# Second matmuls of the last feed-forward: from one pass per token tile behind four gelus to one pass per block right behind its gelu

## The chip, the cores and the metric

The kernel runs on one core of a Trainium2 chip. The metric is the device time of one launch in microseconds (us); lower is better. The inputs and outputs lie in the chip's memory.

## What is computed

The reference is a stack of two gated layers on 4 x 1024 tokens of 256 features. Only its last two steps bear on the change:

```
x = x + jnp.tanh(g_xattn[1]) * _L1_xattn_ref(_layernorm(x, axis=-1), ctx_1024, ctx_1024)
x = x + jnp.tanh(g_ffn[1]) * _L1_ffn_ref(_layernorm(x, axis=-1), ...)
```

The first is softmax attention of 16 heads (depth 16) over 154 keys. The second is a feed-forward whose butterfly stages are linear, so the kernel folds them into its two weight matrices ahead of time:

```
h = jnp.einsum('bsd,dh->bsh', x, W_exp) + b_exp     # 256 -> 1024
h = butterfly(h, up_weights, D_HIDDEN)
h = jax.nn.gelu(h + up_bias, approximate=False)
h = butterfly(h, down_weights, D_HIDDEN)
y = jnp.einsum('bsh,hd->bsd', h, W_con) + b_con     # 1024 -> 256
return y + down_bias
```

What is left of it is y = gelu(x A + a) C + c with A 256 x 1024 and C 1024 x 256. The 1024 hidden units are 8 blocks of 128.

## The kernel before

Five engines each run their own program; they meet at semaphores. There are three stages (first attention, experts, last), and this text is about the last, which fills the span from about 870 us on. It works on halves: h = 0 to 7, each of 512 tokens (4 tiles of 128). x stays on the chip, and each half is updated in place.

All five programs walk one list of units, made by `plan_last`. Its clock is a position n = 20 h + c. At every position one 128 x 512 block of attention weights of half h is made: `scores1` (TensorE, into one of the score banks of PSUM), `exp1` (ScalarE, `ACTIVATE`, L1124), and after every five of them `weigh1` (L652, L647), a ScalarE copy, and `normalize1` (L881, L1536 to L1541). `scores1` of n + 2 is issued at position n and waits for the exp of n - 1, since three banks take turns. Beside that, `beside(h, c)` adds at fixed c:

- the next half's preparation: `peak` units (16 in a half, two PSUM banks each; L846 and L848 on TensorE, then two maxima of 128 x 308 on VectorE, L1521), `peaks` (their transposition, L856), and for h + 2 its layer norm, `turn_q1` and `send_q1`;
- the feed-forward of half h - 1: layer norm `f` (L1180, L1183, L1221 on VectorE, L1621 on GpSimd), `turn_f`, then at c = 9 and at c = 19 a **burst** of four `up` units (hidden blocks 0 to 3 and 4 to 7). Each `up` is six 512-column matmuls (L898: two halves of the contraction times three products of high and low parts), a gelu on ScalarE (L1152), a cast on VectorE (L1569) and a subtraction on GpSimd (L1668) that yield the high and the low part of the hidden block;
- the second matmuls, `out`: one unit per token tile t, 12 matmuls of 256 columns (L911: four blocks times three products) into a bank of its own, and one VectorE addition into x (L1578). They stand at c = 12 to 15 for the burst at 9, and at c = 1 to 4 of the next half for the burst at 19. The first of them waits for the low part of all four blocks.

PSUM banks 4 to 7 are a ring, `wide`, which `peak`, `up`, `out` and the transpositions share in the order of the list. Hidden blocks have four buffers, and the gelu's own output two (`whole`), so the gelu of a block waits for the subtraction of the block two before it. Names of tiles in the trace: `hidden_whole` is `whole`, `hidden` the two parts, `peaks` the maxima, `q_stack` and `k_stack` the stacked queries and keys.

The feed-forward of half 7 stands behind all attention (positions 160 and on); there nothing is left beside it.

## Time and profile before

| what | value |
|---|---|
| median of 3 runs | 1425.98 us (1422.92 to 1426.78) |
| profiled execution, own time | 1429.87 us |
| its span | 1428.1 us |
| TensorE busy | 1148.7 us, 80% |
| VectorE busy | 823.9 us, 58% |
| ScalarE busy | 739.4 us, 52% |
| GpSimd busy | 380.0 us, 27% |
| mean granted TensorE clock | 0.883 of full speed |

The busy times are sums over the whole span, so they hide that the stages have different limits: in the last stage one has to see which engine is waited for in each stretch between two bursts. A granted clock of 1.00 is 2.4 GHz and of 0.50 is 1.2 GHz; a mean between them is the share of either.

### The profile page before, as it was taken

Reading aid. Unit: us, or ns where it says so; the run is one execution under the profiler, and the core shown is the slowest. Engines: PE = TensorE matmul, PEld = TensorE weight load, DVE = VectorE, ACT = ScalarE, POOL = GpSimd, SP = SyncE. Lnnn points to the kernel's source line nnn. Section 1 sums busy time; section 2 is a strip of 40 time slices with the busy share of each in tenths; the row PEclk is TensorE's granted clock in tenths of the full one; section 3 lists DMA queues with packets and bytes.
Section 4 is the critical chain, followed back from the end, with each engine's and each line's share of the span. In section 5 each row is a group of like instructions: output and inputs, shape, how many; then the busy total and the mean of one; then the engine's idle time right before and its main releaser. Section 6 shows DMA issues by size and latency. Waiting matters only on the chain.

```text
span 1428.1 us, 18332 instructions
## 1 busy us (share of the span) xinstructions
PE 1148.7 (80%) x6049; PEld 842.0 (59%) x6049; DVE 823.9 (58%) x2068; ACT 739.4 (52%) x1469; POOL 380.0 (27%) x320
## 2 busy tenths in 40 slices
PE   4788888787774667999699961769888888989887
PEld 3354543543333456888588861637766666767566
DVE  4386687777765554455645434657565565755342
ACT  2786677777862643556656521343443435334521
POOL 3011011011000001566556552103323242321422
PEclk9697999999996999999999995597989998999988
DMA  8214414504103103677557745330403123020000
GB/s 251 78 63 118 115 60 118 173 18 128 51 34 138 71 1 95 157 164 178 169 141 168 187 71 142 98 93 2 112 20 89 43 70 93 17 60 3 15 15 15
DMA packets 89900, 129.77 MB, mean 91 GB/s; under 512 B 20496, under 2 KB 59792, under 8 KB 89552
## 3 DMA queue, kind: packets, MB, share of 16 engines
q1 hardware_dynamic: 77520, 109.73, 25.8%
q0 software_dynamic: 12288, 18.88, 7.6%
q8 instruction: 49, 0.80, 0.2%
q14 instruction: 43, 0.35, 0.1%
HBM read 72.18 MB, written 30.70 MB: 72 GB/s over the span
## 4 chain that ended last, share of the span: by engine, by line
PE 58%; DVE 17%; ACT 10%; issue 5%; DMA 3%; SPq 3%; POOL 3%; POOLq 0%; ACTq 0%; DVEq 0%
PE psum L911 8%; PE psum L741 6%; PE psum L652 5%; PE psum L817 4%; PE psum L629 3%; PE psum L757 3%; PE psum L846 3%; PE psum L776 3%; PE psum L647 3%; PE psum L898 3%; POOL hidden L1668 3%; SPq L1725 2%; PE psum L826 2%; PE psum L618 2%; DVE weights L1281 2%
## 5 line engine op out<-in xcount | busy, mean ns | idle before, releaser
L629 PE MATMUL psum<-q_stack,k_stack 96*128 96x512 f32 (+1 forms) x256 | 130.2, 525 | 70.9 <-ACT weights L1124 29.3
L1616 POOL TENSOR_SCALAR vareps<-moments 128x4 f32<-128x4 f32 x32 | 8.3, 260 | 517.0 <-DVE moments L1183 517.0
L1668 POOL TENSOR_TENSOR hidden<-hidden_whole,hidden 128x512 fp32r<-128x512 f32 x64 | 83.8, 1316 | 203.0 <-DVE hidden L1569 203.0
L1521 DVE TENSOR_REDUCE peaks<-psum 128x2 f32<-128x308 f32 x256 | 105.5, 468 | 46.1 <-PE psum L848 46.0
L1649 POOL DMA_INDIRECT expert_sums<-made,sum_rows x64 | 102.9, 1607 | 101.2 <-DVE made L1491 85.2
L846 PE MATMUL psum<-k_stack,q_stack 96*128 96x256 f32 x256 | 97.6, 443 | 33.9 <-DMA q_stack<-q_stage 11.0
L911 PE MATMUL psum<-w_con_high,hidden 128*128 128x256 f32 x512 | 114.2, 322 | 10.6 <-POOL hidden L1668 10.5
L629 PEld LDWEIGHTS psum<-q_stack,k_stack 96*128 96x128 f32 (+1 forms) x256 | 52.8, 211 | 116.9 <-DVE weights L1281 46.7
L652 PE MATMUL psum<-weights,values 128*32 128x512 f32 x512 | 106.4, 701 | 10.3 <-DVE weights L1281 10.3
L1124 ACT ACTIVATE weights<-psum 128x512 f32<-128x512 f32 x160 | 88.9, 602 | 47.9 <-PE psum L632 23.9
L1281 DVE SCALAR_TENSOR_TENSOR weights<-psum,weights 128x512 f32<-128x512 f32 x160 | 107.1, 679 | 5.4 <-ACT weights L982 5.0
L1641 POOL DMA_INDIRECT got<-rows_scratch,tokens x64 | 70.2, 1097 | 142.5 <-DVE sum_rows L1478 123.3
L1569 DVE CAST hidden<-hidden_whole 128x512 fp32r<-128x512 f32 x64 | 51.1, 799 | 95.1 <-ACT hidden_whole L1152 94.0
L911 PEld LDWEIGHTS psum<-w_con_high,hidden 128*128 128x128 f32 x512 | 91.9, 218 | 23.6 <-POOL hidden L1668 12.6
L982 ACT ACTIVATE weights<-weights 128x512 f32<-128x512 f32 x160 | 101.2, 632 | 1.0
L977 ACT ACTIVATE weights<-weights 128x512 f32<-128x512 f32 x160 | 100.4, 628 | 0.1
L741 PE MATMUL psum<-feat_parts,w_shared_up 128*128 128x512 f32 x384 | 98.4, 406 | 0.0
L846 PEld LDWEIGHTS psum<-k_stack,q_stack 96*128 96x128 f32 x256 | 59.4, 232 | 63.0 <-issue 40.0
L969 ACT ACTIVATE weights<-psum 128x512 f32<-128x512 f32 x128 | 75.9, 593 | 12.2 <-PE psum L629 7.3
L741 PEld LDWEIGHTS psum<-feat_parts,w_shared_up 128*128 128x128 f32 x384 | 71.8, 194 | 14.4
L911 PE MATMUL psum<-w_con_low,hidden 128*128 128x256 f32 x256 | 78.7, 307 | 0.0
L898 PE MATMUL psum<-feats,w_up_high 128*128 128x512 f32 x256 | 77.1, 414 | 1.7 <-DVE feats L1561 1.7
(187 smaller groups left out, 2646.2 us busy)
## 6 DMA issues: line engine op xcount, KB each, us to landing
q_stack<-q_stage SPq DMA_DIRECT2D x192, 128.0 KB, 2.4
expert_w<-in_expert_w SPq DMA_DIRECT2D x64, 384.0 KB
expert_sums<-zeros SPq DMA_DIRECT2D x6, 1408.0 KB, 7.1
fetched<-expert_sums SPq DMA_DIRECT2D x16, 512.0 KB, 4.6
wk_stack<-in_wk SPq DMA_DIRECT2D x16, 384.0 KB, 3.8
rows_scratch<-rows SPq DMA_DIRECT2D x8, 640.0 KB, 3.4
k_raw<-in_k SPq DMA_DIRECT2D x16, 300.0 KB
x<-in_x SPq DMA_DIRECT2D x8, 512.0 KB, 6.7
```

What stands on the lines that cost most here:

```text
L629: T.matmul(to, k[0:row, head, :], q[0:row, head // 2, :], start=True, stop=True).then_inc(scored, 1)
L652: m = T.matmul(to[32 * j:32 * j + 32, :], vals[:, 0, 4 * g + j, :], w[(n + j) % len(w)][:, :], start=True, stop=False, tile_position=(0, 3 ...
L741: m = T.matmul(misc.ap(key, half), w_sgu[:, pw, a:a + P], sh_parts[:, pf, c * HALF:(c + 1) * HALF], start=n == 0 and c == 0, stop=n == 2 a ...
L846: T.matmul(view[:, :, 0:P], q[0:STACK, p, t * P:(t + 1) * P], keys[0:STACK, 2 * p:2 * p + 2, :], start=True, stop=True)
L898: m = T.matmul(wide.ap(key), up_parts[pw][:, c, k * P:(k + 1) * P], feats[:, pf, c, :], start=i == 0 and c == 0, stop=i == 2 and c == CD - 1)
L911: m = T.matmul(wide.ap(key)[:, 0:DIM], hidden[k][:, ph, t * P:(t + 1) * P], con_parts[pw][:, BURST * b + k, :], start=k == 0 and q == 0, s ...
L977: A.activation(weights[n % 9][:, :], weights[n % 9][:, :], ACT.Ln, bias=1.0, scale=1.0 if on_act else -1.0).then_inc(logged, 1)
L982: A.activation(weights[n % 9][:, :], weights[n % 9][:, :], ACT.Exp, scale=-1.0).then_inc(exped, 1)
L1281: V.scalar_tensor_tensor(weights[n % 9][:, :], score_bank[n % 5], 1.0, weights[n % 9][:, :], ALU.add, ALU.max).then_inc(weighted, 1)
L1521: V.tensor_reduce(peaks[h % 2][:, t, 2 * p:2 * p + 2], view, AX.X, ALU.max).then_inc(wide.frees(key, i), 1)
L1649: G.indirect_dma_start(sum_dram[e % SUMS], bass.IndirectOffsetOnAxis(ap=sum_rows[:, e:e + 1], axis=0), made[e % 4][:, :], None, bounds_che ...
L1668: G.tensor_tensor(hidden[k % BURST][:, 1, :], whole[n % 2][:, :], hidden[k % BURST][:, 0, :].bitcast(F32), ALU.subtract).then_inc(hid_spli ...
```

## The change

The unit `out` is now (h, b, k): block k of burst b, all four token tiles, 12 matmuls that wait only for that block's low part. The four tiles are summed over the four blocks in two banks of their own (3 and 4), two tiles to a bank, and VectorE adds each bank to x in one instruction of 128 x 512 when all four blocks are in. The banks come from two places: the score banks go from three to two, so `scores1` now runs one position ahead instead of two (`scores1` of n + 1 at position n, which still waits for the exp of n - 1), and the ring `wide` goes from four to three. `burst` interleaves a burst on TensorE: up 0, up 1, up 2, out 0, up 3, out 1, out 2, out 3. In the burst at c = 9 three of the 16 `peak` units stand between its pieces. `out` units no longer stand at c = 12 to 15 and 1 to 4; `peaks` moves from c = 12 to 13; the list is one half shorter.

```diff
-PEAKS_AT = (1, 1, 1, 1, 2, 1, 2, 2, 1, 3, 1)
+PEAKS_AT = (1, 1, 1, 1, 1, 1, 1, 2, 4, 1, 1, 1)
+
+
+def burst(h, b, between):
+
+    up, out = [("up", h, BURST * b + k) for k in range(BURST)], [("out", h, b, k) for k in range(BURST)]
+    between = [[u] for u in between] + [[]] * 4
+    return up[:2] + between[0] + [up[2], out[0]] + between[1] + [up[3], out[1]] + between[2] + [out[2], out[3]]
...
-        if c == 12:
+            peak = peak[sum(PEAKS_AT[:c - 1]):sum(PEAKS_AT[:c])]
+            units, peak = (units + peak[:1], peak[1:]) if c == 9 else (units + peak, [])
+        if c == 13:
             units.append(("peaks", h + 1))
...
         if c in (9, 19):
-            units += [("up", h - 1, c // 10 * BURST + k) for k in range(BURST)]
-        if 12 <= c < 12 + HT:
-            units.append(("out", h - 1, 0, c - 12))
-    if 2 <= h <= HALVES + 1 and 1 <= c <= HT:
-        units.append(("out", h - 2, 1, c - 1))
-    return units
+            return units + burst(h - 1, c // 10, peak)
+    return units + peak
...
-    for n in range(20 * (HALVES + 2)):
+    for n in range(20 * (HALVES + 1)):
...
-        if n + 2 < len(CHUNKS):
-            plan.append(("scores1", n + 2))
+        if n + 1 < len(CHUNKS):
+            plan.append(("scores1", n + 1))
...
-        score_bank, o_bank, o_bank1 = bank[0:5], bank[5], bank[3]
+        score_bank, o_bank, o_bank1, out_bank = bank[0:5], bank[5], bank[2], bank[3:5]
...
-        wide = Ring(bank[4:8], sems("wide_full", 4), sems("wide_free", 4))
+        wide = Ring(bank[5:8], sems("wide_full", 3), sems("wide_free", 3))
...
-                attention_scores(n, FIRST, 3, exped, q1_stack, k1_stack, ROWS1)
+                attention_scores(n, FIRST, 2, exped, q1_stack, k1_stack, ROWS1)
...
+            def out_part(h, b, k):
+                n = BURST * (2 * h + b) + k
+                if h == 0 and k == 0:
                     T.wait_ge(con_split, 4 + b + 1)
...
+                T.wait_ge(hid_split, n + 1)
+                for t in range(HT):
+                    if k == 0 and t % 2 == 0 and n:
+                        T.wait_ge(out_added, n // BURST * 2 - 1 + t // 2)
                     for q, (ph, pw) in enumerate(PRODUCTS):
...
+                        m = T.matmul(out_bank[t // 2][:, t % 2 * DIM:(t % 2 + 1) * DIM],
+                                     hidden[k][:, ph, t * P:(t + 1) * P], con_parts[pw][:, BURST * b + k, :],
+                                     start=k == 0 and q == 0 and t % 2 == 0,
+                                     stop=k == BURST - 1 and q == 2 and t % 2 == 1)
+                m.then_inc(out_made, 1)
...
+            def out_add(h, b, k):
+                if k == BURST - 1:
+                    n = 2 * h + b
+                    if b == 0:
+                        V.wait_ge(out_biased, h + 1)
+                    V.wait_ge(out_made, BURST * (n + 1))
+                    for two in range(HT // 2):
+                        xs = x[:, HT * h + 2 * two:HT * h + 2 * two + 2, :].rearrange("p i f -> p (i f)")
+                        if b:
+                            V.wait_ge(out_added, 2 * n - 1 + two)
+                        V.scalar_tensor_tensor(xs, out_bank[two], tg[:, 3:4], xs, ALU.mult,
+                                               ALU.add).then_inc(out_added, 1)
```

The first place is TensorE's burst at c = 19 of half 3 and what follows it (`feats` and `w_up` are the operands of `up`, `hidden` and `w_con` those of `out`, `q_stack` those of scores, `k_stack` of peaks). Before:

```order
L898 MATMUL psum<-feats,w_up_high 128x512 x4
L898 MATMUL psum<-feats,w_up_low 128x512 x2
L898 MATMUL psum<-feats,w_up_high 128x512 x2
L629 MATMUL psum<-q_stack,k_stack 128x512
L647 MATMUL psum<-weights_1,values_1 128x512
L629 MATMUL psum<-q_stack,k_stack 128x512
L846 MATMUL psum<-k_stack,q_stack 128x2x128
L848 MATMUL psum<-k_stack,q_stack 128x2x26
L846 MATMUL psum<-k_stack,q_stack 128x2x128
L848 MATMUL psum<-k_stack,q_stack 128x2x26
L911 MATMUL psum<-w_con_high,hidden 128x256 x2
L911 MATMUL psum<-w_con_low,hidden 128x256
```

After, from the last block of the same burst (lines 898, 911, 629, 647, 846 and 848 are now 903, 916, 634, 652, 851 and 853):

```order
L903 MATMUL psum<-feats,w_up_high 128x512 x2
L903 MATMUL psum<-feats,w_up_low 128x512 x2
L903 MATMUL psum<-feats,w_up_high 128x512 x2
L916 MATMUL psum<-w_con_high,hidden 128x256 x2
L916 MATMUL psum<-w_con_low,hidden 128x256
...
L634 MATMUL psum<-q_stack,k_stack 128x512
L652 MATMUL psum<-weights_1,values_1 128x512
L634 MATMUL psum<-q_stack,k_stack 128x512
L851 MATMUL psum<-k_stack,q_stack 128x2x128
L853 MATMUL psum<-k_stack,q_stack 128x2x26
```

Before, scores and weighing followed the four `up` units at once, and the second matmuls came behind them between `peak` units; now all second matmuls of the burst stand ahead of the next scores, and no second matmul follows until the next burst.

The second place is VectorE from the burst at c = 19 (the casts) to the one at c = 9 of the next half. Before:

```order
L1569 CAST hidden<-hidden_whole 128x512 x4
L1521 TENSOR_REDUCE peaks<-psum 128x2 x2
L1578 SCALAR_TENSOR_TENSOR x<-psum,tanh_gates,x 128x256
L1536 RECIPROCAL sums_1<-psum 128x16
L1538 TENSOR_TENSOR att_1<-psum,sums_1 128x256
L1541 SCALAR_TENSOR_TENSOR x<-att_1,tanh_gates,x 128x4x64
L1521 TENSOR_REDUCE peaks<-psum 128x2 x2
L1180 BN_STATS stats<-x 128x6 x4
L1183 BN_AGGR moments<-stats 128x2 x4
```

After:

```order
L1575 CAST hidden<-hidden_whole 128x512 x4
L1587 SCALAR_TENSOR_TENSOR x<-psum,tanh_gates,x 128x512 x2
L1527 TENSOR_REDUCE peaks<-psum 128x2 x2
L1542 RECIPROCAL sums_1<-psum 128x16
L1544 TENSOR_TENSOR att_1<-psum,sums_1 128x256
L1547 SCALAR_TENSOR_TENSOR x<-att_1,tanh_gates,x 128x4x64
L1527 TENSOR_REDUCE peaks<-psum 128x2 x2
L1186 BN_STATS stats<-x 128x6 x4
L1189 BN_AGGR moments<-stats 128x2 x4
```

The four additions of 128 x 256 that stood between maxima are two of 128 x 512 ahead of all of them, behind the burst's last matmul.

## Rows read from the trace of the kernel before

**Rows 1.** Who TensorE waited for, 980 to 1368 us: total us, times, longest.

```profile
PE psum L629 <- ACT weights L1124: 25.9, 13, 3.0
PE psum L846 <- DVE peaks L1521: 9.1, 11, 1.2
```

**Rows 2.** Timeline around a burst at c = 19: start, us, engine, line, idle before.

```profile
1134.10 0.73 PE L898 MATMUL psum<-feats,w_up_high 128*128 128x512 f32 x2
1135.84 1.28 ACT L1152 ACT_TABLE_LOAD   x1 [2.72 <-PE psum L898]
1138.43 1.29 POOL L1668 TENSOR_TENSOR hidden<-hidden_whole,hidden 128x512 fp32r<-128x512 f32 x1 [13.37 <-DVE hidden L1569]
1139.77 0.40 PE L629 MATMUL psum<-q_stack,k_stack 100*128 100x512 f32 x1
1144.04 0.50 PE L629 MATMUL psum<-q_stack,k_stack 100*128 100x512 f32 x1 [3.01 <-ACT weights L1124]
```

**Rows 3.** Busy us of each engine in stretches, then granted clock, DMA share.

```profile
core 0: us, PE busy (x) PEld busy (x) DVE busy (x) ACT busy (x) POOL busy (x), PEclk, DMA share, GB/s
926.00:952.00 26.00, 20.52 (x117) 13.11 (x117) 21.62 (x52) 13.75 (x25) 2.02 (x2) 0.99 0.09 26
960.00:977.00 17.00, 16.25 (x60) 12.26 (x61) 11.05 (x31) 3.87 (x8) 7.76 (x5) 0.50 0.20 65
1083.00:1106.00 23.00, 21.96 (x139) 17.27 (x139) 17.46 (x47) 6.10 (x12) 8.35 (x5) 0.89 0.12 40
1106.00:1119.50 13.50, 11.83 (x52) 9.40 (x52) 8.12 (x14) 7.28 (x10) 5.10 (x4) 0.88 0.00 1
1119.50:1134.00 14.50, 13.45 (x92) 10.06 (x89) 9.01 (x25) 5.79 (x11) 1.27 (x2) 0.94 0.02 5
1134.00:1144.00 10.00, 7.03 (x31) 5.00 (x27) 4.31 (x4) 5.82 (x8) 4.49 (x4) 1.00 0.74 174
1144.00:1168.00 24.00, 22.87 (x142) 17.94 (x142) 17.61 (x47) 6.78 (x13) 8.97 (x6) 0.88 0.32 92
1182.00:1197.50 15.50, 14.45 (x90) 11.01 (x88) 11.40 (x28) 7.37 (x13) 2.00 (x2) 0.87 0.14 42
```

**Rows 4.** VectorE groups (last row: 980 to 1378 us): count, busy, mean ns.

```profile
L1281 DVE SCALAR_TENSOR_TENSOR weights<-psum,weights 128x512 f32<-128x512 f32 x160 | 107.1, 679 | 5.4 <-ACT weights L982 5.0
L1521 DVE TENSOR_REDUCE peaks<-psum 128x2 f32<-128x308 f32 x256 | 105.5, 468 | 46.1 <-PE psum L848 46.0
L1578 DVE SCALAR_TENSOR_TENSOR x<-psum,tanh_gates,x 128x256 f32<-128x256 f32 x64 | 30.1, 475 | 55.2 <-PE psum L911 55.0
L1541 DVE SCALAR_TENSOR_TENSOR x<-att,tanh_gates,x 128x256 f32<-128x256 f32 x26 | 14.5, 557 | 0.9
```

**Rows 5.** Who VectorE waited for, 1098 to 1160 us.

```profile
DVE normed L1221 <- POOL rstd L1621: 1.1, 2, 0.7
```

**Rows 6.** Timeline of half 0, which has no feed-forward beside it, TensorE.

```profile
939.51 0.60 PE L856 MATMUL psum<-ident,peaks 128*16 128x128 f32 x4 [1.25 <-DVE peaks L1521]
950.27 1.06 PE L652 MATMUL psum<-weights,values 128*32 128x512 f32 x8
```

**Rows 7.** The chain that ended last, pieces in order of time: start, us, what.

```profile
1061.02 1.43 PE psum L911 x12
1318.55 1.60 PE psum L898 x6
1344.81 1.60 PE psum L898 x6
1368.78 1.61 PE psum L898 x6
1390.45 7.38 PE psum L898 x24
1417.47 7.47 PE psum L911 x48
```

**Rows 8.** Who TensorE waited for, 1368 to 1428 us.

```profile
PE psum L911 <- POOL hidden L1668: 10.5, 3, 3.9
```

More of the change, by code:

```diff
@@ L272, in norm_units @@
     return [("stats", kind, h), ("rstd", kind, h), ("norm", kind, h)]
-PEAKS_AT = (1, 1, 1, 1, 2, 1, 2, 2, 1, 3, 1)
+PEAKS_AT = (1, 1, 1, 1, 1, 1, 1, 2, 4, 1, 1, 1)
[3 more added lines that the diff above has]
+    return up[:2] + between[0] + [up[2], out[0]] + between[1] + [up[3], out[1]] + between[2] + [out[2], out[3]]
 def beside(h, c):
-    units = []
+    units, peak = [], []
     if h + 1 < HALVES:
@@ L285, in beside @@
             peak = [("peak", h + 1, t, two) for t in range(HT) for two in range(PAIRS // 2)]
-            units += peak[sum(PEAKS_AT[:c - 1]):sum(PEAKS_AT[:c])]
-        if c == 12:
+            peak = peak[sum(PEAKS_AT[:c - 1]):sum(PEAKS_AT[:c])]
+            units, peak = (units + peak[:1], peak[1:]) if c == 9 else (units + peak, [])
+        if c == 13:
             units.append(("peaks", h + 1))
@@ L335, in plan_last @@
         plan += beside_peaks.pop(n, [])
-    plan += [("peaks", 0)] + splits + [("scores1", 0), ("scores1", 1)]
-    for n in range(20 * (HALVES + 2)):
+    plan += [("peaks", 0)] + splits + [("scores1", 0)]
+    for n in range(20 * (HALVES + 1)):
         h, c = divmod(n, 20)
@@ L355 @@
         "project_o": 1, "turn_rows": CD, "gate": 1, "count": 1, "sh_up": 2, "sh_down": 1}
-WIDE = {"turn_q1": CD, "peak": 2, "peaks": 1, "normalize1": 1, "turn_f": CD, "up": 1, "out": 1}
+WIDE = {"turn_q1": CD, "peak": 2, "peaks": 1, "normalize1": 1, "turn_f": CD, "up": 1}
 FUSING = {"inside": 1, "turn_up": 1}
@@ L1123, in exp1 @@
                 A.wait_ge(scored, FIRST + n + 1)
[L1124 removed]
+                A.activation(weights1[n % 6][:, :], score_bank[n % 2], ACT.Exp).then_inc(exped, 1)
             def weigh1(group, part):
@@ L1814, in turn_peaks, with send_out @@
                                     peak_t[a::2, r:r + 1, :].bitcast(F32)).then_inc(max_in[h % 2], 16)
-            def out_tile(h, b, t):
-                if b and t % 2:
-                    tiles = slice(HT * h + t - 1, HT * h + t + 1)
-                    for i in (t - 1, t):
-                        S.wait_ge(*wide.freed(("out", h, b, i)))
-                    S.dma_start(out_view[:, tiles, :], x[:, tiles, :]).then_inc(out_done, 16)
+            def send_out(h, b, k):
+                if b and k == BURST - 1:
+                    for two in range(HT // 2):
+                        tiles = slice(HT * h + 2 * two, HT * h + 2 * two + 2)
+                        S.wait_ge(out_added, 4 * h + 2 + two + 1)
+                        S.dma_start(out_view[:, tiles, :], x[:, tiles, :]).then_inc(out_done, 16)
             load_x(0)
```

38 lines of the change are left out of this document (9 added, 29 removed).

## The prediction

> **What bounds the kernel now.** I read the page first, then who waited for whom on TensorE in the last stage, then the timeline of one half, then busy times by stretch. The change touches nothing ahead of about 910 us. From 980 to 1368 us TensorE waits for two things in the main: 25.9 us in 13 waits for the exp that frees a score bank, the longest 3.0, and 9.1 us in 11 waits for maxima that free a ring bank [rows 1]. The 3.0 us waits stand behind each burst at c = 19. There the four `up` units run from 1134.10 to 1139.77, so 1.42 each; ScalarE loads the gelu's table at 1135.84, when block 0 is in PSUM, and GpSimd finishes the low part of block 0 at 1138.43 + 1.29 = 1139.72 [rows 2]. The next exps stand behind four gelus on ScalarE, which wait for GpSimd, so the third score of TensorE starts only at 1144.04 [rows 2]. So TensorE has nothing to do while the hidden blocks go through three engines, and has their second matmuls to do later.
>
> A half takes 62 us. I cut it into four stretches, with half 3 to 4 as the example [rows 3]: D, the burst at c = 19 up to that late score, 9.9 us; A, from there to the burst at c = 9, 23 to 24; B, from this burst to the transposed maxima (L856), 13.5; C, from there to the next burst, 14.5 in an odd half and 15.5 in an even one (which splits new keys as well). TensorE is busy 91 to 96% in A, B's end and C, but the clock is not full there: 0.89 and 0.88 in A means 2 x 0.11 x 23 = 5 us at 1.2 GHz. VectorE works 17.5 of 23.5 us in A, and 8.1 and 9.0 in B and C. That matters below.
>
> **The change, part by part.** TensorE's instructions are the same in number and kind; an `out` of either kind is 12 matmuls in 1.43 us [rows 7]. Only their place changes, so the question is what each stretch is limited by once the second matmuls (4 x 1.43 = 5.7 us) have left A and C for D and B.
>
> *D.* Three `up` units take 4.25 us, to 1138.35 on the example's clock. Block 0 is ready at 1139.72, a wait of 1.4. Then out 0 (1.43), up 3 (1.42), outs 1 to 3 (4.3): GpSimd takes 1.29 for each low part, TensorE 1.43 for each `out`, so the others are in time. Sum 12.8, and 0.7 for the next score and weighing: 13.5 against 9.9, +3.6. The exp's 3.0 us wait is covered here, since ScalarE has finished the four gelus before TensorE has finished out 3.
>
> *A.* TensorE has 22.0 us busy, of which half of the 5 slow ones is clock: 19.4 at 2.4 GHz. Out go four `out` (5.7) and two of twelve `peak` units (0.9): 12.8 remain. VectorE has 17.5; out go four additions (4 x 0.475 = 1.9) and four maxima (4 x 0.468 = 1.9), in come two additions of 128 x 512. No such one from PSUM into x is in the trace; the nearest is L1281, 0.679 [rows 4]: +1.4. So VectorE has 15.1 us, and it starts only after the burst's last matmul, since the two additions stand ahead of all maxima. With its wait for the reciprocal deviation (0.7 to 1.1 [rows 5]) and about 1 for the first maxima, A is bound by VectorE at 17.0. I add 1.2 for stretches at half clock: 18.2 against 23.5. Bounds: 15.1, and 21.7 if all of A runs at 1.2 GHz, from 960 to 984 us, where half 1's first ten positions (twelve peak units, no `out`) ran at 0.50 for the first 17 us with TensorE 96% busy [rows 3].
> D and A together: 31.7 against 33.4, -1.7, for halves 2 to 6: **-8.5**.
>
> *B.* The burst now holds four `up`, four `out` (11.4), three `peak` (an estimate of 0.47 each, half of VectorE's 2 x 0.468 that pace them now) and, with three ring banks for four, waits of 0.9: 13.7. Behind it VectorE owes two additions (1.4), the maxima of c = 10 to 12 (2.8) and one attention output (three instructions, the longest 0.56: 1.1) before L856 can start: 19.0 against 13.5. In an even half two subtractions of keys stand there as well. Two like them make VectorE's C 11.4 instead of 9.0 [rows 3], so 2 more: 21.
>
> *C.* TensorE has 13.45 busy at 0.94, 12.6 at full clock, less 5.7: 6.9. ScalarE has 5.8 (odd) or 7.4 (even) [rows 3], and with one score in advance instead of two TensorE can't build up a stock before ScalarE's copies. Half 0 shows such a stretch without `out`: from L856 at 939.51 to the end of the last weighing at 951.3 it took 11.8 us [rows 6]. Between 6.9 and 11.8 I take 8.7 for odd halves and, nearer to half 0's (itself even), 11.2 for even ones.
> B and C together: 27.7 against 28.0 in halves 1, 3, 5; 32.2 against 29.0 in halves 2 and 4; half 6, which prepares no keys and queries, as before. Sum -0.9 + 6.4 = **+5.5**.
>
> *Half 7* has no peak units. From burst to burst: 1318.55, 1344.81, 1368.78 [rows 7], 26.3 and 24.0. The first becomes 13.5 + (26.3 - 9.9 - 5.7 = 10.7) = 24.2. The second becomes 12.8 plus what is left of it without matmuls of the feed-forward and without waits: 24.0 - 11.4 = 12.6 with waits, 8 without: 20.8 (25.4 if no wait goes). Sum **-5.4**.
>
> *The end.* From 1368.78 to 1390.45 TensorE does four `up` (5.7), waits 3.9 for the hidden blocks, does the first tile's `out` (1.4), and about 10 us of copy, transposition, layer norm and feature split follow. With the burst whole, these 10 come behind 12.8 + 1.2: 24 against 21.7, +2. From 1390.45 to 1424.94 (= 1417.47 + 7.47) stand the two last bursts, with 10.5 - 3.9 = 6.6 us of waits [rows 7, 8]. They become 16 x 1.43 = 22.9 of matmuls, 3 for a slow clock at their start and none of the long waits, since `out` k has two units of TensorE between it and `up` k: 26 against 34.5, -8.5. Last, two additions of 0.68 follow the last matmul instead of one of 0.475: +0.9. Sum **-5.6**.
>
> *Half 0* gets the shorter score lead with nothing in exchange: 6.9 to 11.8 bounds its stretches too, **+1**.
>
> Sum: -8.5 + 5.5 - 5.4 - 5.6 + 1 = -13. The profiled execution took 1429.87, 3.9 above the median of 1425.98; the difference is taken off the median: **1413 us**.
>
> **What speaks against it: the clock.** Half 0 ran its thin stretch from 926 to 952 us, TensorE 79% busy, at 0.99; half 1 ran a like one at 0.50 from 960 to 977 although TensorE was 96% busy [rows 3]. So a stretch of this kind has run at either level here, and D at 1.00. The change makes A and C thin. The Trainium skill, page "TensorE: Matmul & The Clock Gate", section "A second HAM failure mode: psum-queue depth-cycling", says that small idle times between groups of matmuls, from cycling through PSUM banks, let the clock swing between its two levels. By that rule fewer banks would mean more of it and the rival below would be the forecast; the trace agrees in half 1 and disagrees in half 0.
>
> **The rivals.**
> 1. *Half clock in the thin stretches, slower than before (0.25).* One mechanism: after the burst at c = 19 VectorE paces A, TensorE's clock drops there and stays down up to the next burst, as it did for 17 us in half 1. A costs 21.7 instead of 18.2, five times: +17.5; C has 13.8 us of matmuls at 1.2 GHz against my 8.7 and 11.2, about +4, six times if every time: up to +24. That gives 1430 with A alone and 1454 with both. For it: half 1. Against it: half 0, and that D, which precedes each A, ran at 1.00. It decides from +13 in eleven stretches, 1.2 us each.
> 2. *The waits only move (0.15), 1422 to 1430.* VectorE and ScalarE, which are not sped up, set A, B and C, and the steady halves lose what the end gains: it needs 7 to 8 us more than my -3 for halves 1 to 6, such as 20 for A. For it: TensorE's idle time in my own sum is larger than before (4.2 in A, 5 in B, 2 to 4 in C, against 7 a half).
> 3. *All goes better (0.08), under 1402.* VectorE's wait for the layer norm vanishes, C comes near 6.9 and A near 15.1: -3 and -2 a half, some 1398.
> The forecast, 1402 to 1421, has 0.52.
>
> **How the numbers follow.** A measurement here tells 0.3%, 4.3 us, from no change. Faster by more: 0.52 + 0.08 = 0.60; within: 0.15; slower: 0.25. The range leaves 0.07 below 1401 and about 0.12 above 1436, where rival 1 holds in A and a part of C.
>
> **What would show it right or wrong.** Right: the 3.0 us waits for exps behind the bursts are gone, a wait of about 1.4 for GpSimd's subtraction stands before out 0 at c = 19, that burst is 12 to 13 us long, A is 17 to 19 us with VectorE busy 15 of them, L856 comes 19 us after the start of the burst at c = 9 in odd halves and 21 in even ones, C is 9 and 11, and from the first `up` of half 7 to the end of TensorE it is 26 us. Wrong: a granted clock under 0.8 in A or C, C near 12 in odd halves (the score lead of one), or L856 much later than 21.

## The result: 1.7% slower, and what the profile after shows

The changed kernel takes a median of 1448.76 us (1446.52 to 1452.29, 4 runs) against 1425.22 for the kernel before (4 runs): a ratio of 1.0169, 95% interval 1.0143 to 1.0194. Its profiled execution took 1446.52 us, with a span of 1444.9 against 1428.1. The page of the changed kernel:

```profile
PE 1143.2 (79%) x6049; PEld 825.1 (57%) x6049; DVE 823.1 (57%) x2036; ACT 742.5 (51%) x1469; POOL 373.8 (26%) x320
```

TensorE's busy time fell by 5.5 us and the mean granted clock rose from 0.883 to 0.892. So TensorE was idle for 22.3 us more, and the span grew by 16.8. Who it waited for from 980 to 1391 us, as in [rows 1] (whose two rows are the same up to 1391):

```profile
PE psum L851 <- DVE peaks L1527: 19.1, 22, 2.6
PE psum L634 <- ACT weights L1130: 18.1, 21, 1.0
PE psum L861 <- DVE peaks L1527: 8.8, 6, 2.1
PE psum L916 <- POOL hidden L1677: 7.2, 6, 1.2
```

The 3.0 us waits for exps are gone, as predicted. The waits for maxima are twice as many and twice as long in total, and now the transposition of the maxima (L861) waits too. The timeline of the burst at c = 19 of half 3 (start, us, engine, line, idle before), which answers to [rows 2]:

```profile
1147.45 0.72 PE L903 MATMUL psum<-feats,w_up_high 128*128 128x512 f32 x2
1149.19 1.28 ACT L1158 ACT_TABLE_LOAD   x1 [2.79 <-PE psum L903]
1151.78 1.26 POOL L1677 TENSOR_TENSOR hidden<-hidden_whole,hidden 128x512 fp32r<-128x512 f32 x1 [10.29 <-DVE hidden L1575]
1153.10 0.51 PE L916 MATMUL psum<-w_con_high,hidden 128*128 128x256 f32 x2 [1.20 <-POOL hidden L1677]
```

Three `up` units, 1.20 us of waiting for GpSimd's first low part (1151.78 + 1.26 = 1153.04), then the interleaved rest to 1160.6. The stretches of this half and of the next burst, as in [rows 3] (us, busy times of PE, PEld, DVE, ACT, POOL, clock): D, A with its two pieces, B, C.

```profile
1147.50:1161.10 13.60, 12.40 (x77) 10.62 (x75) 3.89 (x5) 5.81 (x7) 5.13 (x4) 1.00 0.51 117
1161.10:1171.00 9.90, 7.22 (x41) 4.48 (x39) 7.98 (x25) 4.45 (x8) 1.68 (x3) 1.00 0.79 228
1171.00:1183.20 12.20, 10.37 (x47) 7.64 (x48) 8.03 (x17) 2.77 (x5) 6.62 (x3) 0.64 0.07 9
1161.10:1183.20 22.10, 17.59 (x87) 12.12 (x86) 16.01 (x41) 7.22 (x13) 8.30 (x5) 0.80 0.40 107
1183.20:1205.40 22.20, 18.61 (x110) 15.52 (x110) 13.21 (x26) 9.33 (x13) 5.16 (x4) 0.96 0.07 20
1205.40:1215.90 10.50, 8.59 (x42) 3.78 (x42) 7.84 (x20) 6.65 (x12) 1.26 (x2) 0.85 0.07 24
```

D is as predicted, 13.6 against 13.5. A is not: 22.1 against 18.2. VectorE is busy 16.0 us of it, about as forecast (15.1), but idle for 6.1, and the clock is 1.00 in the first 9.9 us and 0.64 in the rest. VectorE's groups in A (last column: idle before them, and who ended it):

```profile
L1527 DVE TENSOR_REDUCE peaks<-psum 128x2 f32<-128x308 f32 x19 | 8.1, 471 | 2.9 <-PE psum L853 2.8
L1547 DVE SCALAR_TENSOR_TENSOR x<-att,tanh_gates,x 128x256 f32<-128x256 f32 x2 | 2.0, 991 | 0.1
L1587 DVE SCALAR_TENSOR_TENSOR x<-psum,tanh_gates,x 128x512 f32<-128x512 f32 x2 | 1.4, 747 | 3.1 <-PE psum L916 3.1
...
L1567 DVE TENSOR_TENSOR feats<-psum,feats 128x512 fp32r<-128x512 f32 x2 | 1.4, 692 | 1.2 <-ACT feats L941 1.1
L1227 DVE TENSOR_SCALAR normed<-x,moments,rstd 128x256 f32<-128x256 f32 x4 | 1.4, 408 | 0.9 <-POOL rstd L1630 0.9
L1542 DVE RECIPROCAL sums<-psum 128x16 f32<-128x16 f32 x2 | 0.5, 253 | 0.9 <-PE psum L886 0.9
```

(The 3.1 before L1587 fell into D. The mean of L1547, the addition of the attention output into x, is of one instruction of 0.49 and one of 1.50 us; the last section says why.) Why the idle time is there, the chain that ended last shows, in order of time (start, us, what):

```profile
1163.44 0.45 PE psum L886 x4
1163.91 0.27 DVE sums L1542
...
1165.15 0.78 DVE peaks L1527 x2
1165.93 1.31 DVE stats L1186 x4
...
1167.99 1.04 POOL rstd L1630
...
1169.12 1.38 DVE normed L1227 x4
1170.51 0.40 DVE peaks L1527
...
1170.94 0.47 PE psum L851
...
1172.75 1.80 PE psum L577 x8
1174.57 0.61 ACT feats L941
1175.20 0.69 DVE feats L1567
...
1176.55 1.50 DVE x L1547
```

The chain goes from TensorE to VectorE to GpSimd to VectorE, back to TensorE, to ScalarE and to VectorE again, where L1547 takes 1.50 us. No engine is full; each is next in turn. The maxima stand in VectorE's queue between the links of this chain (L1527 after the attention output, L1527 after the normed tokens), and TensorE's next `peak` waits for them (0.04 us after the end of L1527 at 1170.90).

The first burst of each half is at c = 9. I add up the stretches over the same bursts in both traces (first `up` to first `up`; the last row but one starts at the burst at c = 19 of half 7, the last at the first `up` of the feed-forward of half 7):

| piece | before | after | difference | predicted |
|---|---|---|---|---|
| up to the first burst | 983.9 | 985.3 | +1.4 | +1 |
| D + A, five times | 167.6 | 176.1 | +8.5 | -8.5 |
| B + C, six times | 167.0 | 179.3 | +12.3 | +5.5 |
| half 7, two stretches | 50.2 | 50.0 | -0.2 | -5.4 |
| next stretch, with the layer norm behind the burst | 21.7 | 24.2 | +2.5 | +2 |
| from there to the end of the span | 37.6 | 30.0 | -7.6 | -7.6 |

The six halves between, 20.8 us longer, in one window each, before and then after:

```profile
984.00:1318.50 334.50, 300.45 (x1675) 232.17 (x1673) 202.67 (x478) 145.28 (x231) 102.69 (x77) 0.91 0.20 54
```

```profile
985.30:1340.70 355.40, 301.73 (x1682) 225.25 (x1681) 204.01 (x460) 147.61 (x231) 99.74 (x77) 0.93 0.19 51
```

TensorE is busy for the same time, 300.5 and 301.7 us, at a slightly higher clock; idle for 34.1 before and 53.7 after. Of the 20.9 us between the two windows 19.6 are idle time.

### The profile page after: what moved, and what is told of

Same layout as the page of the kernel before. It is cut to its first block, busy times and chain, and to the rows that moved or that the text cites. A ratio compares the mean times of both kernels' runs of the same rounds, so it can differ in the third digit from the quotient of the medians.

```text
span 1444.9 us, 18299 instructions
## 1 busy us (share of the span) xinstructions
PE 1143.2 (79%) x6049; PEld 825.1 (57%) x6049; DVE 823.1 (57%) x2036; ACT 742.5 (51%) x1469; POOL 373.8 (26%) x320
## 4 chain that ended last, share of the span: by engine, by line
PE 57%; DVE 20%; ACT 9%; issue 5%; DMA 4%; SPq 3%; POOL 1%; POOLq 0%; DVEq 0%; ACTq 0%
PE psum L916 7%; PE psum L746 6%; PE psum L903 5%; PE psum L657 5%; PE psum L634 4%; PE psum L822 3%; PE psum L762 3%; PE psum L652 3%; PE psum L781 3%; PE psum L851 2%; SPq L1734 2%; PE psum L623 2%; PE psum L831 2%; DVE peaks L1527 2%; PE psum L577 2%
## 5 line engine op out<-in xcount | busy, mean ns | idle before, releaser
L634 PE MATMUL psum<-q_stack,k_stack 96*128 96x512 f32 (+1 forms) x256 | 141.5, 567 | 62.5 <-DVE weights L1287 28.2
L1527 DVE TENSOR_REDUCE peaks<-psum 128x2 f32<-128x308 f32 x256 | 108.4, 472 | 46.8 <-PE psum L853 46.2
L657 PE MATMUL psum<-weights,values 128*32 128x512 f32 x512 | 111.0, 732 | 10.5 <-DVE weights L1287 10.5
L916 PE MATMUL psum<-w_con_high,hidden 128*128 128x256 f32 x512 | 95.5, 287 | 9.6 <-POOL hidden L1677 8.4
L746 PE MATMUL psum<-feat_parts,w_shared_up 128*128 128x512 f32 x384 | 98.3, 406 | 0.0
L916 PEld LDWEIGHTS psum<-w_con_high,hidden 128*128 128x128 f32 x512 | 79.8, 189 | 16.7 <-POOL hidden L1677 11.9
L1158 ACT ACTIVATE hidden_whole<-psum,hidden_bias 128x512 f32<-128x512 f32 x64 | 42.7, 687 | 82.6 <-PE psum L903 70.0
L903 PE MATMUL psum<-feats,w_up_high 128*128 128x512 f32 x256 | 82.8, 423 | 2.8 <-DVE feats L1567 1.5
```

The costliest lines, as they stand in the source:

```text
L634: T.matmul(to, k[0:row, head, :], q[0:row, head // 2, :], start=True, stop=True).then_inc(scored, 1)
L657: m = T.matmul(to[32 * j:32 * j + 32, :], vals[:, 0, 4 * g + j, :], w[(n + j) % len(w)][:, :], start=True, stop=False, tile_position=(0, 3 ...
L746: m = T.matmul(misc.ap(key, half), w_sgu[:, pw, a:a + P], sh_parts[:, pf, c * HALF:(c + 1) * HALF], start=n == 0 and c == 0, stop=n == 2 a ...
L903: m = T.matmul(wide.ap(key), up_parts[pw][:, c, k * P:(k + 1) * P], feats[:, pf, c, :], start=i == 0 and c == 0, stop=i == 2 and c == CD - 1)
L916: m = T.matmul(out_bank[t // 2][:, t % 2 * DIM:(t % 2 + 1) * DIM], hidden[k][:, ph, t * P:(t + 1) * P], con_parts[pw][:, BURST * b + k, :] ...
L1527: V.tensor_reduce(peaks[h % 2][:, t, 2 * p:2 * p + 2], view, AX.X, ALU.max).then_inc(wide.frees(key, i), 1)
```

## The experiments

The kernels below ran on chips where the kernel before took about 1430 us; each ratio is to the kernel before on the same chip.

**The banks alone** (e1 to e3). The kernel before with the change's banks; the second matmuls stay where they are, in the ring.

```diff
-        wide = Ring(bank[4:8], sems("wide_full", 4), sems("wide_free", 4))
+        wide = Ring(bank[5:8], sems("wide_full", 3), sems("wide_free", 3))
...
-                attention_scores(n, FIRST, 3, exped, q1_stack, k1_stack, ROWS1)
+                attention_scores(n, FIRST, 2, exped, q1_stack, k1_stack, ROWS1)
```

e1 has both edits, e2 the first, e3 the second; with the second goes the score lead of one position. Expected of e1:

> The kernel before with the two sets of banks of the change (two score banks with one score in advance, three ring banks) and nothing else: every unit, the second matmuls too, stands where it stood before. Theory of the banks: VectorE's maxima and ScalarE's exps stop TensorE earlier in every stretch; the change lost 23 us although its end gained 5, so the banks alone cost 20 to 28 us, and the waits for maxima go from 9 to about 20 us or more. Theory of the places: it is the move of the second matmuls into the bursts that leaves too little beside VectorE's work; then this kernel is within 5 us of the one before, since the second matmuls still fill its thin stretches.

Of e2:

> The kernel before with three ring banks instead of four. Theory of the banks: of its 20 to 28 us the ring costs the greater part, 12 to 20, since a peak unit takes two banks and three hold one and a half units. Theory of the places: under 4 us.

Of e3:

> The kernel before with two score banks and one score in advance instead of three and two. Theory of the banks: 5 to 10 us, most of it in the 3.0 us waits behind the bursts at c = 19, which grow. Theory of the places: under 3 us.

Measured: e1 1.0149 (1.0102 to 1.0196), e2 1.0147 (1.0112 to 1.0182), e3 1.0004 (0.9982 to 1.0027). The shorter score lead costs nothing that could be measured. A ring of three that the second matmuls share with the maxima costs 1.5%, and the six halves take 348.1 us in e2. So e1 came out as the theory of the banks had it, about 21 us, e3 as that of the places, and e2, some 21 us, just above the 12 to 20 of the banks' theory. The waits of e2 show which banks are missing: `out` now waits for VectorE's additions and attention output.

```profile
PE psum L911 <- DVE x L1578: 4.8, 5, 1.0
PE psum L911 <- DVE att L1538: 2.2, 5, 0.5
```

The changed kernel has the `out` units in banks of their own, so this is no measure of its loss yet; e13 below is.

**The clock** (e4). The changed kernel with two more matmuls at each of c = 2 to 8, into a bank that is idle there; their sums are used by nothing.

```diff
+            def warm(h, c):
+                T.wait_ge(out_added, 4 * (h - 1))
+                for i in range(2):
+                    T.matmul(out_bank[1], k1_stack[h // 2 % 2][0:ROWS1, c, :], q1_stack[h % 2][0:ROWS1, 0, :],
+                             start=True, stop=True)
```

> The changed kernel with two more matmuls of 512 columns at c = 2 to 8 of halves 2 to 7, into an output bank that is idle then, whose result nobody reads: 42 x 2 matmuls of 0.22 us at full clock, 18 us of TensorE work more. Theory of the clock (the changed kernel's stretch A took 22.1 us instead of the forecast 18.2, since its last 12 us ran at 0.64): the granted clock in A goes from 0.80 to over 0.95, and A gets shorter in spite of the added work, by 1 to 3 us a half: 5 to 15 us under the changed kernel. Rival, A is paced by VectorE and the chain of the layer norm whatever the clock: A stays at 22 or grows by up to 3 us, the kernel 0 to 15 us slower than the changed one.

Measured: 1.0127 (1.0097 to 1.0158). The window of A in e4 (us, busy, clock):

```profile
1156.00:1179.00 23.00, 19.30 (x104) 12.99 (x104) 17.31 (x41) 7.11 (x13) 8.35 (x5) 0.93 0.38 103
```

The clock rose from 0.80 to 0.93 and A did not become shorter (23.0 against 22.1). The six halves took 358.2 us. The rival had A right (22 to 25) and the time not: the ratio is no higher than the changed kernel's, and the two intervals overlap. So raising the clock alone, at the price of 14 more matmuls in each A, does not shorten A; D + A went from 176.1 to 177.7. That A is longer by 0.9 goes with one instruction: L1555 here, which is L1547 of the changed kernel, took 2.42 us in this A instead of 1.50.

**The maxima's size** (e5, e6). Both kernels with each maximum over 38 of the 154 keys; everything else stays.

```diff
-                V.tensor_reduce(peaks[h % 2][:, t, 2 * p:2 * p + 2], view, AX.X,
+                V.tensor_reduce(peaks[h % 2][:, t, 2 * p:2 * p + 2], view[:, :, 0:38], AX.X,
```

> The changed kernel with maxima over the first 38 of the 154 keys of each head instead of all (a bound that is smaller than the largest score, so the softmax subtracts less; the work on VectorE is a quarter, the number of instructions and every place and wait are kept). Theory: with three ring banks TensorE walks in step with VectorE's maxima. A maximum goes from 0.47 to some 0.25 us, 20 of them in A and 32 in a half, and A shrinks from 22.1 to 17 or 18 us: 25 us or more under the changed kernel. Rival, A is long because of TensorE's clock and the chain of the layer norm and not because of the maxima: under 8 us.

> The same quarter of maxima in the kernel before, with its four ring banks. Theory: here TensorE and ScalarE set the pace and the second bank pair hides most of a unit's maxima; 3 to 12 us under the kernel before, less than half of what the changed kernel gets from the same cut. Rival: VectorE paces both alike, and both get the same.

Measured: e5, from the changed kernel, 0.9852 (0.9799 to 0.9905); e6, from the kernel before, 0.9876 (0.9818 to 0.9933). The changed kernel gains 3% by it, before 1.2%. A in e5:

```profile
1142.60:1159.20 16.60, 13.62 (x87) 9.26 (x85) 10.70 (x41) 7.11 (x13) 8.34 (x5) 1.00 0.51 143
```

VectorE is 5.3 us less busy (0.9 of it is L1547, at 0.59 us here instead of 1.50) and A is 5.5 us shorter. The clock rose too, from 0.80 to 1.00, but e4 had most of that rise without a shorter A. So A is set by the chain through VectorE, idle links included. The changed kernel gains some 45 us (25 or more were expected) and the kernel before some 18, more than the 3 to 12 expected but less than half of 45. But the six halves still take 324.7 us in e5 against 312.5 in e6, all but 1.2 of it in B + C: the maxima explain the loss in D and A and not the one in B and C.

**The end alone** (e7). The kernel before; only half 7 has its bursts interleaved and its second matmuls block by block, in two score banks that are no longer needed.

```diff
-        if c in (9, 19):
+        if c in (9, 19) and h == HALVES:
+            units += burst(h - 1, c // 10)
+        elif c in (9, 19):
             units += [("up", h - 1, c // 10 * BURST + k) for k in range(BURST)]
```

> The kernel before, with the change in the last two bursts (half 7, behind all attention) alone: there each block's second matmuls follow its gelu, summed in the score banks that nobody uses any more, and the ring keeps its four banks. Theory: the end of the changed kernel took 30.0 us from its first up unit where the one before took 37.7, and nothing else moves: 7 to 8 us under the kernel before. Rival, the shorter end of the changed kernel came from elsewhere (clock, order of arrival): under 3 us.

Measured: 1425.08 us, 0.9943 (0.9916 to 0.9970). The end's gain is real, as expected, and this kernel beats both. From 1391.4 us its span has 28.8 us left against 37.6 before. That it comes from the interleaving is not shown. In e8 and e13 below half 7 has its second matmuls block by block too, but behind all four `up` units, and they have 29.7 and 28.4 us left from the same point. What all of these share is that each block's second matmuls wait for that block alone.

**The placement** (e8, e10, e11). e8 is the changed kernel with its `out` by block at the old positions:

```diff
-            return units + burst(h - 1, c // 10, peak)
+            units += [("up", h - 1, c // 10 * BURST + k) for k in range(BURST)]
+        if 12 <= c < 12 + HT:
+            units.append(("out", h - 1, 0, c - 12))
+    if 2 <= h <= HALVES + 1 and 1 <= c <= HT:
+        units.append(("out", h - 2, 1, c - 1))
```

> The changed kernel with its banks and its second matmuls by block, but these stand where they stood before: at c = 12 to 15 and 1 to 4, with the two additions behind the fourth. Against the changed kernel it undoes the move into the bursts alone. Theory of the banks: the ring of three costs the same in either place, but here the second matmuls need no ring bank any more, so the kernel is 5 to 15 us over the one before, and within 8 us of the changed kernel. Theory of the places: it falls back to the kernel before, within 4 us.

Measured: 1.0013 (0.9979 to 1.0047). D + A takes 160.3 us against 176.1, and the windows of D and A beside those of the changed kernel say why:

```profile
1143.20:1153.10 9.90, 6.93 (x31) 4.99 (x27) 4.10 (x4) 5.84 (x8) 4.49 (x4) 1.00 0.70 162
1153.10:1175.10 22.00, 20.64 (x132) 16.60 (x133) 15.30 (x40) 6.97 (x13) 8.96 (x6) 0.92 0.37 106
```

A takes 22.0 us with the second matmuls in it and 22.1 without them (0.6 of the latter is L1547 at 1.50 us, which took 0.86 in e8). They had been free there, beside VectorE's chain; moved into the burst, they make D 3.7 us longer and A no shorter. Its time is within 4 us of the kernel before, as the theory of the places had it. But B + C was 186.9, longer than in the changed kernel, so e8 alone did not say that all of the loss is the placement.

e10 is a middle way: block 0 right behind the `up` units at 19, blocks 1 to 3 at c = 0, 1, 2, and the burst at 9 as in e8; e11 also draws the latter's blocks forward to c = 10, 11, 12 and 14. Half 7 has whole bursts in both.

> The changed kernel's banks, with second matmuls by block at c = 12 to 15 for the burst at c = 9 as before, but for the one at c = 19 block 0 right behind the four up units and blocks 1 to 3 at c = 0, 1 and 2; in half 7 whole bursts as in the change. Theory: block 0 and 1 fill the 3.0 us in which TensorE waits behind that burst for ScalarE's exps (five times, up to 2.9 us each), while blocks 2 and 3 still lie beside VectorE's work: 8 for the end and 5 to 12 for the waits, 13 to 20 under the kernel before. Rival, what is taken out of A comes back as waits for maxima, as in the change: only the end's 8 remain.

> As the one with the burst at c = 19 thinned, and the second matmuls of the burst at c = 9 at c = 10, 11, 12 and 14 as well. Theory: there TensorE waits 1.2 and 0.5 us for maxima and for a gelu, seven times; blocks 0 and 1 fill these: another 2 to 6 us. Rival: C is thinned as in the change, and it is 0 to 5 us slower than with the burst at c = 19 alone.

Measured: e10 1.0010 (0.9990 to 1.0031), e11 0.9983 (0.9966 to 1.0000). e10 missed both its theory (13 to 20 us faster) and its rival (8); e11 is some 4 us under e10, within the 2 to 6 expected, but their intervals overlap. The waits of e10, 980 to 1391 us:

```profile
PE psum L862 <- DVE peaks L1538: 25.1, 22, 2.6
PE psum L645 <- ACT weights L1141: 8.0, 7, 3.0
```

Matmuls drawn forward into the wait for exps shorten that one, and the wait for maxima grows in its place: from 980 to 1330 us e8 has 20.7 us for exps and 11.0 for maxima, e10 has 4.5 and 25.1.

**More maxima in the burst at 9** (e12). The changed kernel with six `peak` units between the pieces of that burst instead of three, and seven in A instead of ten.

```diff
-PEAKS_AT = (1, 1, 1, 1, 1, 1, 1, 2, 4, 1, 1, 1)
+PEAKS_AT = (1, 1, 1, 1, 0, 1, 0, 1, 7, 1, 1, 1)
```

> The changed kernel with six peak units between the pieces of the burst at c = 9 instead of three, and three fewer in A (seven, with the one ahead of the burst, instead of ten). Theory: VectorE, idle for 9 of the 13 us of a burst and then in arrears, is what makes the changed kernel longer; three units (2.8 us of maxima) out of A make A 2 to 3 us shorter and the burst 1.4 longer, 5 to 12 us under the changed kernel over seven halves. Rival, A is held by the chain of the layer norm and not by the sum of VectorE's work: A stays, the burst grows, and the kernel is 3 to 10 us slower than the changed one.

Measured: 1.0067 (1.0036 to 1.0098), 1% under the changed kernel's ratio. A in e12:

```profile
1158.80:1174.00 15.20, 12.16 (x74) 7.81 (x72) 12.37 (x35) 7.11 (x13) 7.05 (x5) 1.00 0.56 155
```

Three units fewer make A 6.9 us shorter, where 2 to 3 were expected: 2.3 for each unit, whose two maxima take 0.94 of VectorE. L1547 at 0.90 instead of 1.50 us is 0.6 of it, and the clock is 1.00 instead of 0.80; the rest was not taken apart. Most of it returns in B + C (207.9), and 2.1 us of six halves are left as a gain; another 6.9 stand ahead of the first burst, of one execution each.

**Exps ahead of the gelus** (e9). The kernel before with e7's end, and with the exp of position 20 (h + 1) issued ahead of the burst at c = 19, so that it does not stand behind four gelus.

```diff
+        if c == 19 and n + 1 < len(CHUNKS):
+            plan.append(("exp1", n + 1))
         plan += beside(h, c)
```

> The kernel before with the end of the change (half 7) and, in every half, the exp of c = 20 ahead of the gelus of the burst at c = 19 instead of behind them. Theory: the third score behind the burst then waits for nothing, the 3.0 us waits move to the second matmuls, which wait for block 3 (ready 0.7 us later than that score starts now), so most of the 3.0 comes back: 8 for the end and 1 to 5 more, 9 to 13 under the kernel before. If the waits were the exps' alone, it would be 8 + 15 = 23.

Measured: 1420.30 us, 0.9933 (0.9908 to 0.9958), 9.6 us under the kernel before, as expected, and the fastest here that computes everything. Almost all of it is the end's gain (e7: 0.9943). The waits for exps fell from 25.8 us in e7 to 8.4, and others came (980 to 1391 us; of the wait for GpSimd, e7 has 3.7):

```profile
PE psum L921 <- POOL hidden L1704: 10.2, 5, 3.7
PE psum L639 <- ACT weights L1146: 8.4, 7, 2.9
PE psum L856 <- DMA q_stack<-q_stage: 7.5, 3, 3.0
```

**What the other 13 us are** (e13 to e16). Over halves 1 to 6 e8 was 12.6 us longer than before, and it has the ring of three and the new places of the maxima. e13 is e8 with the maxima where they were; e14 is the kernel before with the new places of the maxima alone.

```diff
-PEAKS_AT = (1, 1, 1, 1, 1, 1, 1, 2, 4, 1, 1, 1)
+PEAKS_AT = (1, 1, 1, 1, 2, 1, 2, 2, 1, 3, 1)
...
-        if c == 13:
+        if c == 12:
             units.append(("peaks", h + 1))
```

> The kernel of e8 (banks of the change, second matmuls block by block at the positions of before) with the maxima also at the positions of before: the change's banks and its sums by block, nothing moved. In the six halves from the first burst at c = 9 to the second burst of half 6, before took 334.6 us, after 355.4, e8 347.2 and e2 (ring of three, second matmuls and maxima in it) 348.1. Theory: what e8 has left is the new place of the maxima (two units from A to B and C, where VectorE owes the additions and the attention output too); then this one takes 334 to 339 us there, and the span is some 10 us under e8's 1431.0, ratio 0.990 to 0.995 through the end's gain. Rival: the ring of three costs it, also without the second matmuls in it; then 345 us or more there and a ratio of 0.999 to 1.003.

> The kernel before with the change's places of the maxima alone (nine units up to c = 8, one ahead of the burst at 9, three behind it, then one each at 10 to 12, the transposition at 13). If the maxima's place costs: D + A shorter by 5 to 9 us over five halves, B + C longer by 12 to 20, sum +7 to +12, ratio 1.005 to 1.009. If the ring costs instead: both change against each other and the sum of the six halves stays within 3 us of 334.6, ratio 0.998 to 1.002.

e15 and e16 are the changed kernel with one of its two whole bursts taken apart; here e15:

```diff
-            return units + burst(h - 1, c // 10, peak)
+            if c == 19 or h == HALVES:
+                return units + burst(h - 1, c // 10, peak)
+            units += [("up", h - 1, k) for k in range(BURST)]
+        if 12 <= c < 12 + HT and h < HALVES:
+            units.append(("out", h - 1, 0, c - 12))
```

> The changed kernel with its interleaved burst at c = 19 alone (and in half 7, both); the burst at c = 9 is again four first matmuls with the second ones at c = 12 to 15. D + A then as in the changed kernel (176 us over five halves). If both placements cost alike, B + C falls from 179 to 171 to 175, since the second matmuls fill C, and the ratio is 1.010 to 1.014. If the whole loss of the placement is in D and A, B + C stays at 179 or more (e8 had 186.9) and the ratio is 1.014 to 1.020.

> The mirror image: the changed kernel with its interleaved burst at c = 9 (and in half 7, both), the burst at c = 19 again four first matmuls with the second ones at c = 1 to 4. A was 22.1 us in the changed kernel without the second matmuls and 22.0 in e8 with them, so D + A should fall from 176.1 to e8's 160 us. If the theory that the burst at c = 19 is what costs holds, B + C stays at 179 and the ratio is 1.003 to 1.007. If the waits for exps behind the plain burst and a later slow clock take it back, D + A is 168 or more and the ratio above 1.010.

All by the same measure; the last but one column is from the burst at c = 19 of half 6, where the six halves end, to the end of the span:

| kernel | burst at 9 | burst at 19 | D + A | B + C | six halves | from there to the end | ratio |
|---|---|---|---|---|---|---|---|
| before | | | 167.6 | 167.0 | 334.6 | 109.6 | |
| e14, maxima's places | | | 158.9 | 179.7 | 338.6 | 111.7 | 1.0039 (1.0012 to 1.0067) |
| e13, banks and blocks | spread | spread | 171.9 | 170.5 | 342.4 | 95.6 | 1.0000 (0.9974 to 1.0027) |
| e8, and maxima's places | spread | spread | 160.3 | 186.9 | 347.2 | 98.3 | 1.0013 (0.9979 to 1.0047) |
| e16 | whole | spread | 164.1 | 180.3 | 344.4 | 96.2 | 1.0011 (0.9979 to 1.0042) |
| e15 | spread | whole | 176.3 | 187.0 | 363.3 | 104.5 | 1.0191 (1.0133 to 1.0248) |
| changed kernel | whole | whole | 176.1 | 179.3 | 355.4 | 104.2 | 1.0169 (1.0143 to 1.0194) |

The ratios say it most clearly: with the burst at 19 whole, 1.0169 and 1.0191; with it spread, 1.0011 and 1.0013, whichever way the burst at 9 stands. **The whole burst at c = 19 is the loss, 1.6 to 1.8%.** The kernels with it spread are level with the kernel before for two reasons that cancel: their six halves are 8 to 13 us longer, and what follows is 11 to 14 us shorter. In the changed kernel only 5.4 us of that are left, since the burst at 19 costs there too: the stretch behind it takes 24.2 us, and 18.2 in e16.

The rest is in the spans, each of one execution, so a few us are not significant (25 runs of the kernel before on the chip of e13 to e16 took 1420.3 to 1436.2 us): the banks +7.8 (e13), the maxima's places +4.8 (+4.0 in e14), the whole burst at 9 -2.8, the one at 19 +11.0, together 20.8. In the other order, by e15, the one at 19 is +16.1 and the one at 9 -7.9. Not all of this is waiting. Of the +11.0 from e16 to the changed kernel TensorE's busy time has 4.6, and of the +16.1 from e8 to e15 it has 8.8 (304.6 to 313.4 us, at a clock of 0.90 and 0.88). And 3.0 of the 11.0, 6.2 of the 16.1, go with L1547 and the lines that answer to it, which took that much longer in sum; the last section has them.

e13 missed the expectation for its theory, its halves lie between the two, and its ratio is the rival's. e14 has D + A and B + C as expected for the maxima's places, but a smaller sum (+4.0 against +7 to +12). e15 has the ratio (1.014 to 1.020) and the B + C (179 or more) of its second case: the loss is not shared by the burst at 9. e16's D + A was 164.1 where 160 was expected, its B + C 180.3 against 179, and its ratio a little under. TensorE's waits in e15 and then in e16, 980 to 1330 us:

```profile
PE psum L855 <- DVE peaks L1531: 26.3, 26, 2.6
PE psum L638 <- ACT weights L1134: 7.7, 10, 0.9
```

```profile
PE psum L638 <- ACT weights L1134: 26.9, 18, 3.0
PE psum L865 <- DVE peaks L1531: 8.8, 6, 2.1
PE psum L855 <- DVE peaks L1531: 4.6, 7, 1.0
```

The two waits stand for each other. Where the exps' 3.0 us are waited for behind the plain burst, there is little waiting for the `peak` units behind it (4.6 us); where they are filled with second matmuls, the maxima are waited for (26.3). It is not that VectorE works off its queue during the wait: it is busy for 4.1 us in D of e8 and 3.9 in D of the changed kernel. Behind the plain burst the second matmuls stand between the `peak` units, and TensorE does them while VectorE is behind.

## Why the prediction was wrong

**The failed step is A.** I took A as VectorE's busy time (15.1) and two waits, with 1.2 for the clock: 18.2, and so -8.5 over five halves for D and A. VectorE's busy time was nearly right (16.0, of which 1.0 is L1547 at 1.50 us). But I took it as if its work could follow with gaps of 1.9 us at most, and it is a chain that goes through three other engines and back, with 6.1 us of idle time on VectorE itself. A even went past my upper bound of 21.7, at a clock of 0.80 and not at half, and the prediction gives no full working for that bound. The row to see it by was there: VectorE had 17.5 of 23.5 us in A before [rows 3], so it was idle for 6 us with TensorE 95% busy, and I let this idle time vanish together with the second matmuls. e8 against the changed kernel shows that it stays: 22.0 with them and 22.1 without. A came under what I forecast only with three `peak` units fewer in it, in e12 (15.2).

**D** was right: 13.6 against 13.5, its wait 1.20 against 1.4. Since A gave nothing back, D's growth was a loss as a whole.

**B + C** was right in direction: 28.8 to 29.0 in odd halves against 27.7, 32.6 and 32.7 in even ones against 32.2. Of the miss of 6.8 us, 1.6 are in the base (I took the odd halves' stretch before as 28.0 throughout, and half 1 had 25.0), and 3.7 are the odd halves, some 1.2 each: C took 9.0 there against 8.7 in my sum, the rest is B. The cost itself I put on VectorE's debts behind a whole burst; e16 against e8 and the changed kernel against e15 show no cost of the whole burst at 9 (-2.8 and -7.9 us), and the maxima's new places (e14: B + C +12.7, D + A -8.7) make it longer.

**Half 7** was wrong: I let its waits vanish with the bursts whole (-5.4), and it stayed at 50.0. Behind the bursts exps are waited for again, one score ahead instead of two, and its waits from 1313 to 1391 us are 8 us in sum:

```profile
PE psum L634 <- ACT weights L1130: 4.0, 4, 1.0
PE psum L916 <- POOL hidden L1677: 2.4, 2, 1.2
PE psum L577 <- DVE normed L1227: 1.8, 1, 1.8
```

**The end** was right in each term: +2.5 against +2 and -7.6 against -8.5 + 0.9. What I did not see is that the blocks alone, not interleaved, bring as much (28.4 us in e13 against 30.0) and make the stretch before it shorter (18.1 against 24.2). The additions of 128 x 512 took 0.75 against the 0.68 taken from [rows 4]. Its chain, from the last but one burst:

```profile
1414.91 6.87 PE psum L903 x18
...
1436.19 4.43 PE psum L916 x36
1440.64 0.75 DVE x L1587
```

**The rivals.** The time lies in the range of rival 1, half clock in the thin stretches, but its mechanism is not the cause. The clock in A did fall, to 0.80: it was 1.00 up to 1171 us, 0.52 in the next two, 1.00 again from 1175 to 1177, and 0.50 from 1179 on. Over the six halves it rose from 0.91 to 0.93. The Trainium skill's page "TensorE: Matmul & The Clock Gate", section "A second HAM failure mode: psum-queue depth-cycling", says that short idle times between groups of matmuls make the clock swing between its two levels; the trace agrees in A and not over the six halves. The stretch of half 1 that the prediction counts for that rule does not bear it out: from 956 to 960 us TensorE did nothing at all, the clock was 0.67 there, and it stayed at 0.50 up to 977 with TensorE busy without a gap from 964 on. TensorE's busy time in the six halves grew by 1.3 us only, and e4 raised A's clock without shortening it. What happened is rival 2, the waits only move, with a larger price than the 1422 to 1430 I gave it: I had it end where A takes 20, and A took 22.1. Its condition stood in my own sum (TensorE's idle time larger than before), and I gave it 0.15.

**What stays open.** How much of A is the chain and how much the ring of three: no run had the burst at 19 whole with a ring of four. Why the banks alone (e13) still lengthen the six halves by 7.8 us: TensorE is busy 3.6 us longer there at a clock of 0.90 against 0.91, which leaves 4.2 us of idle time, about what two executions may differ by. Whether the GpSimd addition that holds up L1547 could stand elsewhere: no run moved it. And why the burst at 9 may be whole at no price while the one at 19 may not: that three `peak` units stand inside the first and none in the second, and that the chain of attention output and layer norm follows the second, fits e12, but no run had maxima inside the burst at 19.

## What to carry to other kernels

Work that a full engine does beside another engine's chain is free where it stands. Before moving it, follow the chain that ended last through that stretch: if it goes from engine to engine and would be as long without the work, taking the work away shortens nothing, and the idle time of the engine that is next in line (VectorE, 6 of 23.5 us) is the sign of it. A wait that is filled with such work can come back as a wait for another engine at the place that the work has left; fill it only with work that hid no other wait where it stood. And take a change apart by its ideas before crediting one: here the block-by-block sums, with no burst interleaved, leave 28.4 to 29.7 us behind the last bursts' start against 37.6 before, as much as with the interleaving (28.8 and 30.0), and the end alone brings 0.6% (0.9943, 0.9916 to 0.9970).

## What the runs showed of the hardware

The same instruction of VectorE, L1547 of 128 x 256 into x, took 0.485 us by its median of eight between 1070 and 1177 us, and 1.50 at 1176.55, while GpSimd ran an addition of 128 x 1024 from 1175.40 to 1177.77. It ended at 1178.05, 0.28 us behind GpSimd. In the last stage of all 18 traces the instruction (its line differs) stands 576 times. It took over 0.6 us 68 times, up to 2.62, each time beside such an addition (65) or a subtraction of 128 x 512 (3), and each time it ended 0.28 or 0.29 us after GpSimd's instruction did; with nothing of GpSimd beside it, it never took more than 0.49. Ten more stood beside such an addition for 0.44 us or less and took 0.60 at most. So in the 68 it waits for GpSimd's instruction to end, and what it costs depends on how they fall together. From 985 us on these delays sum to 1.9 us in the kernel before, 5.0 in the changed one, 7.7 in e4, 7.6 in e15 and 2.0 in e16.

In A the granted clock was 1.00 in the first 9.9 us with TensorE 73% busy (7.22 us), and 0.64 in the next 12.2 with 85% (10.37): the busy share alone does not say how much work was done, since the same matmuls take longer at the lower level. At the end of the changed kernel 18 matmuls of L903 took 6.87 us at 1414.91, at a clock of 0.61, and 18 more 4.18 us at 1428.99, at 1.00.
